# First convolution of each pass: one contiguous run over the padded rows instead of rows of 64 out of 66

## The chip, the cores and the metric

The kernel runs on one core of a Trainium2 chip. The metric is device time in microseconds (us), the median of several executions of the whole program. Engines are named as the profile names them: PE is TensorE's matmul, PEld its weight load, DVE is VectorE, ACT is ScalarE, POOL is GpSimd, SP is SyncE.

## The reference, cut to what matters

Three residual steps of two 3x3 convolutions with 64 channels on 16 images of 64 x 64, and behind them one attention block with matrix products of 64 channels. Only the two convolutions matter here:

```
for _ in range(3):
    t = relu(conv(x, w1) + b1)          # 3x3, SAME padding, 64 -> 64 channels
    x = x + 1/3 * (conv(t, w2) + b2)
return relu(x)
```

All is float32. The changed code computes `conv(x, w1)`, called conv0 below; `conv(t, w2)` is conv1.

## The kernel before, in words

**Layout.** An image has 32 groups of two rows each: the 64 channels of the even rows stand on partitions 0 to 63, those of the odd rows on partitions 64 to 127. A group has 64 columns. The tiles `x_hi` and `x_lo` hold an image in two parts (`x_hi` the value rounded to the fp32r type, `x_lo` what is left), with `PADDED` = 66 elements for each group: one zero, 64 pixels, one zero. So an image is 32 x 66 elements to a partition, with no hole between the groups.

**conv0** (`convolve_conv0`, on PE). The output `t` has 33 groups (`SKEWED`), shifted by one row against the groups of x. They are made in five parts of 7, 7, 7, 6 and 6 groups (`CONV0_SIZES`), each in one PSUM bank. A part sums over two stacks (the x group above and the one below) and over three columns xx = 0, 1, 2 of the filter. Each of these six takes three matmuls in the helper `three`: hi x hi, hi x lo and lo x hi (lines 889 to 891), so 18 matmuls a part. In the first part one stack has a group less (its x group lies outside the image), and so in the last part. A matmul before the change reads 64 of each 66 elements (7 rows of 64 with a pitch of 66, shifted by xx), and writes 7 x 64 = 448 contiguous elements of PSUM.

**What follows conv0.** ACT takes each part out of its bank through a ReLU into `t_eo` (`drain_conv0`, lines 488 to 493), even and odd columns apart. DVE turns `t_eo` into `v_all` in two sets (`transform_t`, lines 716 to 731): groups 0 to 20 after part 2, the rest after part 4. conv1 (line 930) multiplies `v_all` on PE, in fp32, in two halves: the first half needs only the first set. Its results go by ACT to `m`, by DVE to `dx`, by an accumulating DMA of POOL into `x_res`, and by ACT and DVE into `x_hi` and `x_lo` again.

**Order.** One round of the loop treats a pair of images, in six passes that alternate between the two images: conv0 in five parts, then conv1 in two halves (7 numbers a pass, `NC` = 42 in a round). There are 8 rounds, so 48 passes. Every engine runs its own instructions in program order and waits on semaphores. Between the convolutions of round i the attention of the pair before is put in by a table (`LATE`), by the number after which a piece comes. Its last pieces on ACT are the `FINISH` steps (line 561), which wait until a store from the same one of two output buffers is done (`stored`, line 387 issues the stores). The last of them stand at numbers 34 and 35, the end of the fifth pass and the first part of the sixth. The three banks for convolutions are used in turn, and PE waits with a part until ACT has emptied the bank three parts before (`bank_free`).

Of the kernel before, what the change touches and what calls it, by code (L numbers as in the profile page):

```python
# [35 lines left out]
IMAGES, CH, ROWS, COLS = 16, 64, 64, 64  # L36
# [8 lines left out]
PADDED = COLS + 2  # L45
# [31 lines left out]
def img_of(n):  # L77

    return PASS[n] % 2


def step_of(n):

    return PASS[n] // 2
# [17 lines left out]
def groups_of(n):  # L102

    if is_conv1(n):
        return half_of(n) * HALF_GROUPS, HALF_GROUPS
    return sum(CONV0_SIZES[:PART[n]]), CONV0_SIZES[PART[n]]


CONV_BANKS = 3
RING = 4  # L110
UNITS = [3 if is_conv1(n) else 1 for n in range(NC)]
UNIT = [sum(UNITS[:n]) for n in range(NC)]
# [67 lines left out]
def i_is(i, value):  # L180

    return isinstance(i, int) and i == value


def conv_attention_kernel(nc, x, w1, b1, w2, b2, qkv_w, o1_w, o2_w, kln_w, kln_b, vln_w, vln_b, out):
# [4 lines left out]
    with ctx:  # L190
# [6 lines left out]
        def pair_of(name, shape, dt=F32):  # L197
            return [sb(f"{name}{k}", shape, dt) for k in range(2)]
# [5 lines left out]
        x_hi = pair_of("x_hi", [P, GROUPS, PADDED], F32R)  # L204
        x_lo = pair_of("x_lo", [P, GROUPS, PADDED], F32R)
# [4 lines left out]
        m = pair_of("m", [P, 6 * PLANE])  # L210
# [49 lines left out]
        conv_ps = banks[0:CONV_BANKS]  # L260
# [177 lines left out]
        def _(act):  # L438
# [37 lines left out]
            def drain_conv0(i, n):  # L476
                g0, size = groups_of(n)
                act.wait_ge(conv_ready, i * NU + UNIT[n] + 1)
                if PART[n] == 0:
                    if i_is(i, 0) and n == 0:  # L480
                        act.wait_ge(consts_made, 3)
                    else:

                        act.wait_ge(v_made, i * NH + PASS[n] * HALVES)
                at = conv_ps[UNIT[n] % CONV_BANKS][:, 0:size * COLS].rearrange("p (j m s) -> p j s m", s=2, m=COLS // 2)
                to = t_eo[:, g0:g0 + size, :, 1:ROW - 1]
                if g0 == 0:
                    nc.scalar.activation(to[0:CH, 0:1], at[0:CH, 0:1], ACT.Relu, bias=b1_col[0:CH, :])
                    at, to = at[:, 1:size], to[:, 1:size]
                elif g0 + size == SKEWED:  # L490
                    nc.scalar.activation(to[CH:P, size - 1:size], at[CH:P, size - 1:size], ACT.Relu, bias=b1_col[CH:P, :])
                    at, to = at[:, 0:size - 1], to[:, 0:size - 1]
                nc.scalar.activation(to, at, ACT.Relu, bias=b1_col[:, :]).then_inc(drained, 1)  # L493
# [74 lines left out]
            def iteration(i, attends, splits, first=False):  # L568
                for n in range(NC):
                    if is_conv1(n):  # L570
                        drain_conv1(i, n)
                    else:
                        drain_conv0(i, n)
                    for number in REFRESH_AT[n]:
                        refresh_hi(i, number)
                    if not first:
                        for number in REFRESH_AT.get(NC + n, ()):
                            refresh_hi(i - 1, number)
                    if first:
                        set_up(n)  # L580
                    if attends:
                        attention(i - 1, LATE[n], RING_USES)
                    if not splits:
                        attention(i, EARLY_LAST.get(n, []), RING_LAST)
                    if splits and n in X_SPLIT[0]:
                        act.wait_ge(f_written, i * 2 * HALVES + HALVES)
                        copy_x(i + 1, 0, X_SPLIT[0][n])
                        split_x_hi(i + 1, 0, X_SPLIT[0][n])
                    if not first and n in X_SPLIT[1]:
                        act.wait_ge(f_written, i * 2 * HALVES)  # L590
                        copy_x(i, 1, X_SPLIT[1][n])
                        split_x_hi(i, 1, X_SPLIT[1][n])
# [266 lines left out]
        def _(pe):  # L859
# [27 lines left out]
            def three(ps, lhs, rhs, first, last):  # L887

                mm(ps, lhs[0], rhs[0], start=first, stop=False)  # L889
                mm(ps, lhs[0], rhs[1], start=False, stop=False)  # L890
                return mm(ps, lhs[1], rhs[0], start=False, stop=last)  # L891

            def convolve_conv0(i, n):
                img, step = img_of(n), step_of(n)
                g0, size = groups_of(n)
                if step == 0:

                    pe.wait_ge(x_split, i * 4 + 2 * img + 1 + (g0 + size >= HALF_GROUPS))
                else:

                    pe.wait_ge(x_ready, i * NR + (PASS[n] - 2) * HALVES + 1 + (g0 + size > HALF_GROUPS))
                bank_free(i, UNIT[n])
                hi, lo = x_hi[img], x_lo[img]
                top, bottom = g0 == 0, g0 + size == SKEWED
                for nth, stack in enumerate((1, 0) if top else (0, 1)):
                    skip_first, skip_last = int(top and stack == 0), int(bottom and stack == 1)
                    ps = conv_ps[UNIT[n] % CONV_BANKS][:, skip_first * COLS:(size - skip_last) * COLS]
                    groups = slice(g0 + stack - 1 + skip_first, g0 + stack - 1 + size - skip_last)
                    for xx in range(K):
                        at = stack * K + xx  # L910
                        cols = slice(xx, xx + COLS)
                        last = three(ps, (w_hi[:, at, :], w_lo[:, at, :]),
                                     (hi[:, groups, cols], lo[:, groups, cols]),
                                     nth == 0 and xx == 0, nth == 1 and xx == K - 1)
                last.then_inc(conv_ready, 1)

# [17 lines left out]
            def bank_free(i, unit):  # L934

                if not (i_is(i, 0) and unit < CONV_BANKS):
                    pe.wait_ge(drained, i * NU + unit - CONV_BANKS + 1)
# [102 lines left out]
            def iteration(i, attends, splits, first=False):  # L1040
                for n in range(NC):
                    if is_conv1(n):
                        convolve_conv1(i, n)
                    else:
                        convolve_conv0(i, n)
                    if first:
                        set_up(n)
                    if attends:
                        attention(i - 1, LATE[n], RING_USES)
                    if not splits:  # L1050
                        attention(i, EARLY_LAST.get(n, []), RING_LAST)
# [27 lines left out]
```

## Time and profile before

| | |
|---|---|
| median of 3 runs | 1622.37 us (1621.98 to 1623.78) |
| profiled execution, first to last instruction (its span) | 1619.8 us |
| PE busy | 1581.7 us, 98% of the span |
| PEld busy | 1372.0 us, 85% |
| DVE busy | 1090.7 us, 67% |
| ACT busy | 751.2 us, 46% |

The profile is of one execution. The page gives no other time for it than its span; the 2.6 us by which the median of the runs is longer lie before the first and behind the last instruction, and in the variation from run to run. Busy times of matmuls overlap, since one starts before the one ahead of it is through; what a stream of matmuls costs is read from the distance between starts.

### The profile page before, as it was taken

What the parts mean: (1) busy time and instruction counts of PE and PEld (TensorE: products, weight loads), DVE (VectorE), ACT (ScalarE), POOL (GpSimd) and SP (SyncE); (2) the same over time, 40 slices, a digit from 0 to 9 for tenths busy, and PEclk for the clock granted to TensorE, in tenths of its full rate; (3) what the DMA queues carried; (4) which work ended last, traced back from release to release, by engine and by line L of the source; (5) the groups of instructions that cost most, each with busy time, mean ns of one, the idle gap of its engine ahead of it and who ended that gap; (6) DMA issues with size and microseconds to landing.
All of it is one profiled execution on the core that took longest, in us unless ns stands there. A gap on an engine that the chain in (4) does not pass through costs nothing.

```text
span 1619.8 us, 25740 instructions
## 1 busy us (share of the span) xinstructions
PE 1581.7 (98%) x9339; PEld 1372.0 (85%) x9339; DVE 1090.7 (67%) x2060; ACT 751.2 (46%) x1322; POOL 85.9 (5%) x107
## 2 busy tenths in 40 slices
PE   7999999999999999999999999999999999999975
PEld 6999988888988889888898888988898879988862
DVE  5565687556875577765767667775587665876574
ACT  4333544436443464435643446433464334543454
POOL 0000000000000000000000000000000000000000
PEclk9999999999999999999999999999999999999997
DMA  6212332333322234122421235122531233112312
GB/s 114 53 26 53 53 53 40 62 57 53 66 40 53 53 55 77 27 52 53 80 52 27 52 66 92 27 39 49 90 60 27 40 59 59 27 27 53 69 37 52
DMA packets 149190, 85.98 MB, mean 53 GB/s; under 512 B 136652, under 2 KB 136652, under 8 KB 149068
## 3 DMA queue, kind: packets, MB, share of 16 engines
q0 software_dynamic: 13824, 50.34, 17.3%
q1 hardware_dynamic: 135164, 33.82, 11.3%
q8 instruction: 83, 1.36, 0.3%
q14 instruction: 39, 0.32, 0.1%
q10 hardware_dynamic: 80, 0.15, 0.0%
HBM read 17.17 MB, written 16.78 MB: 21 GB/s over the span
## 4 chain that ended last, share of the span: by engine, by line
PE 93%; DVE 3%; ACT 2%; issue 1%; DMA 1%; SPq 0%; ACTq 0%; DVEq 0%
PE bank L930 30%; PE bank L889 18%; PE bank L891 16%; PE bank L890 16%; PE bank L977 4%; PE bank L989 4%; PE bank L1023 2%; PE bank L1036 2%; DMA out<-y_out 0%; SPq L387 0%; PE bank L1007 0%; DVE rstd L791 0%; ACT g L541 0%; DVE x_lo L652 0%; ACT x_in L536 0%
## 5 line engine op out<-in xcount | busy, mean ns | idle before, releaser
L889 PE MATMUL bank<-x_hi,w_hi 128*128 128x448 f32 (+2 forms) x1440 | 526.3, 365 | 3.5 <-DVE x_lo L652 3.3
L930 PE MATMUL bank<-v_all,fw 128*128 128x256 f32 x2304 | 517.1, 382 | 1.0 <-DVE v_all L731 0.6
L891 PE MATMUL bank<-x_hi,w_lo 128*128 128x448 f32 (+2 forms) x1440 | 509.3, 354 | 0.0
L890 PE MATMUL bank<-x_lo,w_hi 128*128 128x448 f32 (+2 forms) x1440 | 508.6, 353 | 0.0
L930 PEld LDWEIGHTS bank<-v_all,fw 128*128 128x128 f32 x2304 | 431.7, 190 | 73.7 <-ACT m L506 9.7
L889 PEld LDWEIGHTS bank<-x_hi,w_hi 128*128 128x128 f32 x1440 | 272.0, 189 | 48.3 <-issue 22.8
L891 PEld LDWEIGHTS bank<-x_hi,w_lo 128*128 128x128 f32 x1440 | 271.5, 189 | 15.2
L890 PEld LDWEIGHTS bank<-x_lo,w_hi 128*128 128x128 f32 x1440 | 271.6, 189 | 13.6
L493 ACT ACTIVATE t_eo<-bank,b_col 128x384 f32<-128x384 f32 (+2 forms) x240 | 141.6, 590 | 301.5 <-PE bank L891 300.9
L716 DVE TENSOR_TENSOR steps_q<-t_eo 128x1344 f32<-128x1344 f32 x96 | 119.9, 1249 | 193.4 <-ACT t_eo L493 193.4
L506 ACT ACTIVATE m<-bank 128x512 f32<-128x512 f32 x192 | 114.2, 602 | 167.7 <-PE bank L930 167.6
L434 POOL DMA_DIRECT2D x_res<-dx x96 | 82.4, 859 | 1481.7 <-DVE dx L762 1481.7
L744 DVE TENSOR_TENSOR sums<-m 128x512 f32<-128x512 f32 x96 | 66.3, 691 | 129.7 <-ACT m L506 129.7
L773 DVE TENSOR_TENSOR x_lo<-x_res,x_hi 128x1024 fp32r<-128x1024 f32 x64 | 78.2, 1222 | 106.6 <-ACT x_hi L519 106.6
L784 DVE TENSOR_REDUCE rstd<-g 128x64 f32<-128x512 f32 x128 | 84.4, 680 | 33.9 <-ACT g L541 33.8
L536 ACT ACTIVATE kv<-bank 128x512 f32<-128x512 f32 x120 | 72.7, 606 | 19.7 <-PE bank L977 19.7
L509 ACT ACTIVATE m<-bank,b_third 128x256 f32<-128x256 f32 x96 | 46.1, 480 | 71.7 <-PE bank L930 71.6
L989 PEld LDWEIGHTS bank<-kv 128*65 128x65 f32 x960 | 68.3, 141 | 12.6 <-DVE kv L797 7.4
L541 ACT ACTIVATE g<-bank 128x512 f32<-128x512 f32 x128 | 78.5, 613 | 0.0
L797 DVE TENSOR_TENSOR kv<-kv,rstd 128x512 f32<-128x512 f32 x120 | 76.7, 677 | 0.0
L989 PE MATMUL bank<-kv 128*65 128x65 f32 x960 | 69.0, 225 | 7.0 <-DVE kv L797 7.0
L977 PE MATMUL bank<-kvw,f 64*128 64x128 f32 x1024 | 73.9, 288 | 0.6 <-ACT f L523 0.6
(104 smaller groups left out, 1358.8 us busy)
## 6 DMA issues: line engine op xcount, KB each, us to landing
x_res<-dx POOLq DMA_DIRECT2D x96, 512.0 KB, 4.6
x_in<-in_x SPq DMA_DIRECT2D x64, 256.0 KB, 7.3
out<-y_out SPq DMA_DIRECT2D x120, 128.0 KB, 2.7
out<-v_all SPq DMA_DIRECT2D x8, 128.0 KB, 2.7
x_res<-in_L_conv_w ACTq DMA_DIRECT2D x1, 144.0 KB, 2.8
x_res<-in_L_conv_w SPq DMA_DIRECT2D x1, 144.0 KB, 4.6
b_col<-in_L_conv_b SPq DMA_DIRECT2D x4, 0.2 KB, 2.8
g<-in_L_conv_o_w SPq DMA_DIRECT2D x3, 16.0 KB
```

Of the source, the lines that this page charges most:

```text
L434: nc.gpsimd.dma_start(x_res[img][:, HALF_PX * h:HALF_PX * (h + 1)], dx[h][:, :], accum_op=ALU.add).then_inc(x_added[h], 16)
L493: nc.scalar.activation(to, at, ACT.Relu, bias=b1_col[:, :]).then_inc(drained, 1)
L506: nc.scalar.activation(to[:, BANK * part:BANK * (part + 1)], bank[:, :], ACT.Copy, scale=H_STEP).then_inc(drained, 1)
L541: nc.scalar.activation(squares[k % 2][:, :], ps[:, :], ACT.Square).then_inc(proj_taken, 1)
L716: vec.tensor_tensor(q, later, earlier, ALU.subtract).then_inc(v_parts, 1)
L784: vec.tensor_reduce(rstd[img][:, k, :], squares[k % 2][:, :].rearrange("p (h d) -> p h d", d=HD), AX.X, ALU.add).then_inc(squares_summed, 1)
L889: mm(ps, lhs[0], rhs[0], start=first, stop=False)
L890: mm(ps, lhs[0], rhs[1], start=False, stop=False)
L891: return mm(ps, lhs[1], rhs[0], start=False, stop=last)
L930: last = mm(ps, fw[:, q, 1 - stack, :], v_all[:, KEPT.index(q), g0 + stack:g0 + stack + size, :], start=stack == 0, stop=stack == 1)
L977: last = mm(ps[:, KV * j:KV * (j + 1)], f[img][rows, at], kvw[rows, :], start=True, stop=True)
L989: last = mm(outer_ps, rows[:, at, :], rows[:, at + 1, :], start=(k == 0 and j == 0), stop=(k == PROJ - 1 and j == PX_BANK - 1))
```

## The change

conv0's matmuls read one run without holes and write one: for 7 groups 7 x 66 - 2 = 460 elements, for 6 groups 394, for 5 groups 328. The run starts at column xx of its first group. The results of the two elements between one group and the next are written to PSUM too, and nobody reads them. So a group now has a pitch of 66 in the bank (7 x 66 = 462 of its 512 elements), and ACT's instructions read 64 out of each 66. Number, order and waits of the instructions stay.

```diff
@@ drain_conv0 (ACT)
-                at = conv_ps[UNIT[n] % CONV_BANKS][:, 0:size * COLS].rearrange("p (j m s) -> p j s m", s=2, m=COLS // 2)
+                at = conv_ps[UNIT[n] % CONV_BANKS][:, 0:size * PADDED].rearrange(
+                    "p (j w) -> p j w", w=PADDED)[:, :, 0:COLS].rearrange("p j (m s) -> p j s m", s=2)
@@ convolve_conv0 (PE)
-                hi, lo = x_hi[img], x_lo[img]
+                hi, lo = (t[img].rearrange("p j w -> p (j w)") for t in (x_hi, x_lo))
                 top, bottom = g0 == 0, g0 + size == SKEWED
                 for nth, stack in enumerate((1, 0) if top else (0, 1)):
                     skip_first, skip_last = int(top and stack == 0), int(bottom and stack == 1)
-                    ps = conv_ps[UNIT[n] % CONV_BANKS][:, skip_first * COLS:(size - skip_last) * COLS]
-                    groups = slice(g0 + stack - 1 + skip_first, g0 + stack - 1 + size - skip_last)
+                    rows = size - skip_first - skip_last
+                    run = rows * PADDED - 2
+                    ps = conv_ps[UNIT[n] % CONV_BANKS][:, skip_first * PADDED:skip_first * PADDED + run]
+                    start = (g0 + stack - 1 + skip_first) * PADDED
                     for xx in range(K):
                         at = stack * K + xx
-                        cols = slice(xx, xx + COLS)
+                        run_at = slice(start + xx, start + xx + run)
                         last = three(ps, (w_hi[:, at, :], w_lo[:, at, :]),
-                                     (hi[:, groups, cols], lo[:, groups, cols]),
+                                     (hi[:, run_at], lo[:, run_at]),
                                      nth == 0 and xx == 0, nth == 1 and xx == K - 1)
```

The first place is on PE, in the first part of the first pass, where stack 1 (7 groups) goes over to stack 0 (6 groups). A row is line, operation, output and inputs, and partitions x elements of the moving operand. Before:

```order
L889 MATMUL bank<-x_hi,w_hi 128x448
L890 MATMUL bank<-x_lo,w_hi 128x448
L891 MATMUL bank<-x_hi,w_lo 128x448
L889 MATMUL bank<-x_hi,w_hi 128x384
L890 MATMUL bank<-x_lo,w_hi 128x384
L891 MATMUL bank<-x_hi,w_lo 128x384
```

After:

```order
L890 MATMUL bank<-x_hi,w_hi 128x460
L891 MATMUL bank<-x_lo,w_hi 128x460
L892 MATMUL bank<-x_hi,w_lo 128x460
L890 MATMUL bank<-x_hi,w_hi 128x394
L891 MATMUL bank<-x_lo,w_hi 128x394
L892 MATMUL bank<-x_hi,w_lo 128x394
```

Nothing moved; 448 became 460 and 384 became 394, and the lines are numbered one higher.

The second place is on PE too, at the end of the first pass: the last matmuls of conv0 (5 groups) and conv1 behind them. Before:

```order
L889 MATMUL bank<-x_hi,w_hi 128x320
L890 MATMUL bank<-x_lo,w_hi 128x320
L891 MATMUL bank<-x_hi,w_lo 128x320
L930 MATMUL bank<-v_all,fw 128x256 x24
L873 MATMUL bank<-ident,g 128x128
```

After:

```order
L890 MATMUL bank<-x_hi,w_hi 128x328
L891 MATMUL bank<-x_lo,w_hi 128x328
L892 MATMUL bank<-x_hi,w_lo 128x328
L933 MATMUL bank<-v_all,fw 128x256 x24
L874 MATMUL bank<-ident,g 128x128
```

320 became 328. conv1 stays as it was, 24 matmuls a pass in the program.

## Rows read from the trace of the kernel before

**Rows 1.** The page: busy time of each engine, share of the span, instructions.

```profile
PE 1581.7 (98%) x9339; PEld 1372.0 (85%) x9339; DVE 1090.7 (67%) x2060; ACT 751.2 (46%) x1322; POOL 85.9 (5%) x107
```

**Rows 2.** The page: chain that ended last, by engine and by line.

```profile
PE 93%; DVE 3%; ACT 2%; issue 1%; DMA 1%; SPq 0%; ACTq 0%; DVEq 0%
PE bank L930 30%; PE bank L889 18%; PE bank L891 16%; PE bank L890 16%; PE bank L977 4%; PE bank L989 4%; PE bank L1023 2%; PE bank L1036 2%; DMA out<-y_out 0%; SPq L387 0%; PE bank L1007 0%; DVE rstd L791 0%; ACT g L541 0%; DVE x_lo L652 0%; ACT x_in L536 0%
```

**Rows 3.** Waits of PE: line, what for, us in total, times, longest.

```profile
PE bank L989 <- DVE kv L797: 7.0, 2, 5.7
PE bank L930 <- DVE v_all L731: 0.6, 2, 0.4
```

**Rows 4.** Groups by line and shape: count, busy us, mean ns of one.

```profile
L930 PE MATMUL bank<-v_all,fw 128*128 128x256 f32 x2304 | 517.1, 382 | 1.0 <-DVE v_all L731 0.6
L889 PE MATMUL bank<-x_hi,w_hi 128*128 128x448 f32 x720 | 278.5, 387 | 3.5 <-DVE x_lo L652 3.3
L889 PE MATMUL bank<-x_hi,w_hi 128*128 128x384 f32 x576 | 202.8, 352 | 0.0
L889 PE MATMUL bank<-x_hi,w_hi 128*128 128x320 f32 x144 | 45.0, 313 | 0.0
L889 PEld LDWEIGHTS bank<-x_hi,w_hi 128*128 128x128 f32 x1440 | 272.0, 189 | 48.3 <-issue 22.8 <-ACT t_eo L493 4.9
```

**Rows 5.** Timeline of PE, first pass: start, us until its end, line, shape.

```profile
10.03 0.58 PE L890 MATMUL bank<-x_lo,w_hi 128*128 128x448 f32 x1
12.64 0.54 PE L891 MATMUL bank<-x_hi,w_lo 128*128 128x448 f32 x1
...
14.64 0.37 PE L889 MATMUL bank<-x_hi,w_hi 128*128 128x448 f32 x1
18.18 0.37 PE L891 MATMUL bank<-x_hi,w_lo 128*128 128x448 f32 x1
...
25.23 0.34 PE L889 MATMUL bank<-x_hi,w_hi 128*128 128x384 f32 x1
30.09 0.31 PE L889 MATMUL bank<-x_hi,w_hi 128*128 128x320 f32 x1
31.28 0.31 PE L891 MATMUL bank<-x_hi,w_lo 128*128 128x320 f32 x1
31.43 8.79 PE L930 MATMUL bank<-v_all,fw 128*128 128x256 f32 x40
```

**Rows 6.** Chain in order of time, first pass: start, us, line, count.

```profile
31.59 10.36 PE bank L930 x48
```

**Rows 7.** Windows in the first pass: busy us (count) by engine, then PEclk, DMA.

```profile
14.60:18.20 3.60, 3.60 (x20) 3.26 (x18) 1.46 (x2) 2.68 (x4) 0.00 (x0) 1.00 0.19 35
25.20:31.40 6.20, 6.20 (x37) 6.18 (x37) 5.67 (x11) 3.32 (x4) 0.00 (x0) 1.00 0.76 146
31.60:41.90 10.30, 10.30 (x48) 8.76 (x47) 7.27 (x22) 4.13 (x9) 0.40 (x1) 1.00 0.37 60
```

**Rows 8.** Timeline of DVE, first pass: transform of the first set, first and last.

```profile
26.17 1.55 DVE L716 TENSOR_TENSOR steps_q<-t_eo 128x1344 f32<-128x1344 f32 x1
...
30.08 0.85 DVE L731 SCALAR_TENSOR_TENSOR v_all<-steps_q 128x672 f32<-128x672 f32 x1
```

**Rows 9.** Timeline of a sixth pass (round 6 of 8), from its first matmul to conv1.

```profile
1134.40 0.48 PE L889 MATMUL bank<-x_hi,w_hi 128*128 128x448 f32 x1
1137.48 1.23 ACT L561 ACTIVATE y_out<-y 128x512 f32<-128x512 f32 x2 [1.76 <-DVE y L824]
1138.30 8.46 SPq L387 DMA_DIRECT2D out<-y_out  x6
1144.55 0.66 ACT L561 ACTIVATE y_out<-y 128x512 f32<-128x512 f32 x1 [5.19 <-DMA out<-y_out]
1145.37 0.66 ACT L561 ACTIVATE y_out<-y 128x512 f32<-128x512 f32 x1 [0.16 <-DMA out<-y_out]
1145.93 0.62 ACT L493 ACTIVATE t_eo<-bank,b_col 128x448 f32<-128x448 f32 x1
1146.44 1.05 ACT L523 ACTIVATE f<-x_res 128x1024 f32<-128x1024 f32 x1
1147.39 0.62 ACT L493 ACTIVATE t_eo<-bank,b_col 128x448 f32<-128x448 f32 x1
1148.05 1.56 DVE L716 TENSOR_TENSOR steps_q<-t_eo 128x1344 f32<-128x1344 f32 x1 [7.51 <-ACT t_eo L493]
1151.97 0.85 DVE L731 SCALAR_TENSOR_TENSOR v_all<-steps_q 128x672 f32<-128x672 f32 x1
1152.95 10.62 PE L930 MATMUL bank<-v_all,fw 128*128 128x256 f32 x48
```

**Rows 10.** Waits of ACT for stores: us in total, times, longest.

```profile
ACT y_out L561 <- DMA out<-y_out: 37.4, 11, 5.7
```

## The prediction

> **What bounds the kernel now.** I read the busy shares first, then the chain that ended last, then PE's waits, then the distance between the starts of matmuls. PE is busy for 98% of the span, DVE for 67%, ACT for 46% [rows 1]. The chain agrees: 93% of it is PE, and conv0's three lines hold 18 + 16 + 16 = 50% of it, some 810 us [rows 2]. PE waits for nearly nothing: its longest wait in total is 7.0 us, and for conv1's input it waits 0.6 us [rows 3]. So a nanosecond on a conv0 matmul counts 4320 times: each of the three lines has 720 matmuls of 448 elements, 576 of 384 and 144 of 320 [rows 4], which makes 2160, 1728 and 432.
>
> What one costs is the distance of starts [rows 5]:
> - 448 elements: from 14.64 to 18.18 are 17 steps, 208.2 ns each
> - 384: from 25.23 to 30.09 are 27 steps, 180.0 ns each
> - 320: from 30.09 to 31.28 are 8 steps, 148.8 ns each
> - conv1: 48 matmuls of 256 elements in 10.36 us, 215.8 ns each [rows 6]
>
> The granted clock is 1.00 in all these stretches [rows 7], the level of 2.4 GHz. The weight load does not set the distance: one takes 189 ns [rows 4], yet 320-element matmuls follow each other in 148.8. conv1 has 24 matmuls a pass in the program and 48 in the trace (2304 over 48 passes [rows 4]), so an fp32 matmul is run in two, and 256 elements in 215.8 ns are two array cycles an element (213.3 ns) and 2.5 ns over. This is a contiguous read, and it runs at the clock. conv0 does not: at one cycle an element, 448 elements would be 186.7 + 2.5 = 189.2 ns, and the row says 208.2. The excess is 19.0 ns for 7 rows, 17.5 for 6 (162.5 to 180.0), 13.0 for 5 (135.8 to 148.8): 2.6 to 2.9 ns a row.
>
> The Trainium skill's "TensorE: Matmul & The Clock Gate", section "Back-to-back issue gap", gives elements / 2.4 + 2.5 ns for one matmul at the full clock. By that rule the conv1 row agrees with two runs over its elements, and the conv0 row does not.
>
> **The open question.** All rows of conv0 have 64 elements, so the trace fits two readings equally well. In one, each of the 7 rows costs about 2.7 ns where the read jumps over the two pads. In the other, an fp32r element costs 0.46 ns instead of 0.417, in whatever pattern: (208.2 - 2.5) / 448 = 0.459, (180.0 - 2.5) / 384 = 0.462, (148.8 - 2.5) / 320 = 0.457. For the first speaks that the only contiguous stream, conv1, shows no excess; against it, that conv1 takes its elements at half the rate, so a limit of supply would not show there. In the first nine matmuls, from 10.03 to 12.64, 7 steps take 372.9 ns each [rows 5], just 448 elements at the lower level of 1.2 GHz with no excess (the level is read from the distance alone here). So the excess is no fixed number of array cycles; it lies in the supply, which both readings allow. I take the first, since a supply limited by its mere rate would be 0.459 / 0.417 = 1.10 times the array's cycle, a ratio for which I see no reason, where an interruption at each jump needs none.
>
> **The change part by part.**
> - *Elements added.* 12, 10 and 8 a matmul: 2160 x 12 + 1728 x 10 + 432 x 8 = 46,656. At 0.4167 ns, +19.4 us.
> - *Jumps removed.* In the first reading all excess goes: 2160 x 19.0 + 1728 x 17.5 + 432 x 13.0 ns = 41.0 + 30.2 + 5.6 = 76.8 us. Net -57.4 us, or 194.2 ns for 460, 166.7 for 394, 139.2 for 328. Bounds: nothing removed and the rate kept is 46,656 x 0.46 = +21.5 us; all removed is -57.4.
> - *ACT's read of the bank.* 64 out of each 66 instead of contiguous groups; it already steps by two elements, with as many instructions. I take zero. No row shows a pitch of 66 in PSUM. Were a 448-element read 0.1 us longer, a fifth of its 0.62 us [rows 9], ACT with 46% has room, except in the sixth passes (below), where two such reads and DVE's start behind them would cost some 0.2 us in each of six rounds, 1.2 us.
> - *What no longer hides.* DVE's transform of the first set runs under parts 3 and 4. In the first pass it ends at 30.08 + 0.85 = 30.93, and conv1 starts at 31.43 [rows 5, 8]: 0.50 us to spare. Parts 3 and 4 shrink by 27 x 13.3 + 9 x 9.6 ns = 0.45 us, so it is just hidden still; I charge nothing for the six passes of round 1. In the sixth pass of round 6 it is not hidden. ACT stands 5.19 us in a FINISH step until a store lands, drains part 1 at 1145.93 and part 2 only at 1147.39; DVE ends at 1152.82, and conv1 starts at 1152.95 [rows 9], 0.13 us later, about what a semaphore needs. This chain hangs on a DMA that was issued at 1138.30, near the start of the pass at 1134.40 [rows 9], and on work ahead of that start, not on PE's matmuls in between. What conv0 saves in this pass, 45 x 14.0 + 36 x 13.3 + 9 x 9.6 ns = 1.2 us, PE then waits at line 930. ACT waits for stores 37.4 us in all, 11 times [rows 10]: with 5.19 and 0.16 us in this pass, that is six passes of some 5.3 us and a remainder. They are those of rounds 2 to 7; in the first there is no attention beside the convolutions, and the eighth has another order. Loss 6 x 1.15 = 6.9 us. Lower bound of the loss: only what parts 3 and 4 save, 6 x 0.4 = 2.4 us.
>
> **Sum.** -57.4 + 6.9 = -50.5 us. The profiled execution's span is 1619.8 us, so its span should be 1569.3; the 2.6 us to the median of the runs stay, which gives 1572. Own range of this case: 1560 (the lower loss, 4.5 us less, and 1.7 ns a matmul more gained than the rounded starts show, 7.3 us) to 1585 (3 ns a matmul stay with the run, about the price of one jump, 4320 x 3 ns = 13 us).
>
> **Rivals.**
> 1. *The rate is the limit, not the jump (slower).* 46,656 elements more at 0.46 ns: +21.5 us, 1644. The point that decides is the distance of two 460-element starts: below 208.2 ns the change gains, and at this rate it is 460 x 0.459 + 2.5 = 213.6 ns. For it speaks the equal fit above, and that no contiguous fp32r read is in the trace; against it conv1's exact two cycles and the odd ratio. Chance 0.14.
> 2. *The jump costs only a part of the excess.* If half is rate and half jump, -76.8 / 2 + 19.4 = -19 us, with some 1 us lost at waits, 1604; this case reaches from 1585 to 1619. Chance 0.16.
> 3. *No net change.* The excess removed equals the elements added (a quarter of it removed): within 0.2%, which is 3.2 us and about what a measurement of this kernel can tell. Chance 0.03.
>
> 4. *The excess belongs to the matmul, not to its rows (slower).* Something at the change from one fp32r matmul to the next costs 13 to 19 ns, and stays; then only the added elements count, +19.4 us, 1642. Against it: the excess falls with the rows, 19.0, 17.5, 13.0, and is 0 in the first nine matmuls. Chance 0.04.
>
> The gap rule of "TensorE: Matmul & The Clock Gate" in the Trainium skill ("Back-to-back issue gap") goes with rival 4: it counts elements alone, whatever the pattern, so that 12 more can only cost 5 ns. The page "SBUF — State Buffer" in the Trainium skill, section "Specifications", says that each crossing to a new line of 16 bytes pays a penalty; a run of 460 crosses lines as the rows did, so by that rule too there is little to gain, as in rival 1. No row here tells crossings from jumps.
>
> **How the numbers follow.** The forecast case has 0.63, the partial one 0.16, no change 0.03, slower 0.14 + 0.04 = 0.18. The predicted time is that of the forecast case, 1572. The range takes in its own range and the partial case, 1560 to 1619, which holds 0.79. Faster by over 0.2% is 0.63 + 0.16 = 0.79, same 0.03, slower 0.18.
>
> **What the next profile would show.** Starts of 460-element matmuls 194 ns apart, of 394 167 and of 328 139: the first reading; 214, 184 and 153: the rate; 211, 182 and 152: rival 4. Waits of line 933 (conv1) for v_all of some 1.1 us in the sixth passes, near 7 us in all instead of 0.6. ACT's drains at 0.62 us as before. conv1 still at 215.8 ns. The prediction is wrong if a contiguous run keeps an excess that grows with its length, or if the shorter conv0 exposes DVE in more passes than the sixth.

## The result, and the profile after

The changed kernel takes 1625.15 us (median of 20 runs, 1623.38 to 1629.04) against 1622.38 us before (20 runs). The ratio is 1.0016, with a 95% interval of 1.001 to 1.0023: 2.6 us slower, and within the 0.2% that I called no change. I had forecast 1572 us, with a chance of 0.03 for this.

Ahead of everything else stands the distance of starts. Timeline of PE in the first pass of the changed kernel (start, us until its end, line, shape), the places of [rows 5]:

```profile
14.48 0.37 PE L890 MATMUL bank<-x_hi,w_hi 128*128 128x460 f32 x1
18.03 0.37 PE L892 MATMUL bank<-x_hi,w_lo 128*128 128x460 f32 x1
...
25.10 0.34 PE L890 MATMUL bank<-x_hi,w_hi 128*128 128x394 f32 x1
29.93 0.31 PE L890 MATMUL bank<-x_hi,w_hi 128*128 128x328 f32 x1
31.28 9.01 PE L933 MATMUL bank<-v_all,fw 128*128 128x256 f32 x41
```

From 14.48 to 18.03 are 17 steps, 208.8 ns each, where rows of 448 took 208.2. From 25.10 to 29.93 are 27 steps of 178.9 ns (180.0 before), and 9 steps of 150.0 ns to 31.28 (148.8 before). Forecast were 194.2, 166.7 and 139.2. The jumps are gone, and most of the excess is still there: 14.6, 12.2 and 10.8 ns above the forecast, of the 19.0, 17.5 and 13.0 that were to go. What a whole pass costs is read from the starts of conv1, in the chain that ended last, in order of time (start, us, line, count). Before, and behind it the changed kernel, three passes between the two lines of each:

```profile
87.45 10.36 PE bank L930 x48
170.13 10.36 PE bank L930 x48
```

```profile
87.39 10.36 PE bank L933 x48
170.21 10.36 PE bank L933 x48
```

conv1 takes 10.36 us in both, as in [rows 6]. A pass takes 27.56 us before and 27.61 after, so the 90 matmuls of conv0 in it cost 0.05 us more (0.14 over the three passes). Over 48 passes that would be 2.2 us, an estimate from these three, and nearly the whole of the 2.6 us.

The page of the changed kernel, busy time of each engine:

```profile
PE 1585.9 (98%) x9339; PEld 1374.2 (85%) x9339; DVE 1090.1 (67%) x2060; ACT 750.9 (46%) x1322; POOL 85.9 (5%) x107
```

Against [rows 1] PE is busy 4.2 us longer, DVE and ACT as long to 0.6 us. The span is 1622.7 us, 2.9 more than before. PE's waits for conv1's input, among the waits of PE (us in total, times, longest), and ACT's drain of 448 elements, among the groups by line and shape:

```profile
PE bank L933 <- DVE v_all L732: 0.2, 1, 0.2
```

```profile
L494 ACT ACTIVATE t_eo<-bank,b_col 128x448 f32<-128x448 f32 x96 | 61.0, 636 | 178.4 <-PE bank L892 178.4
```

The waits that I expected behind a shorter conv0 are not there, since conv0 is not shorter (0.2 us, 0.6 in [rows 3]). The drain with a pitch of 66 takes 636 ns, the same group before 635.

### The profile page after: what moved, and what is told of

Same layout as the page of the kernel before. It is cut to its first block, busy times and chain, and to the rows that moved or that the text cites. A ratio compares the mean times of both kernels' runs of the same rounds, so it can differ in the third digit from the quotient of the medians.

```text
span 1622.7 us, 25740 instructions
## 1 busy us (share of the span) xinstructions
PE 1585.9 (98%) x9339; PEld 1374.2 (85%) x9339; DVE 1090.1 (67%) x2060; ACT 750.9 (46%) x1322; POOL 85.9 (5%) x107
## 4 chain that ended last, share of the span: by engine, by line
PE 93%; ACT 3%; DVE 2%; issue 1%; DMA 0%; SPq 0%; ACTq 0%; DVEq 0%
PE bank L933 30%; PE bank L890 18%; PE bank L891 16%; PE bank L892 16%; PE bank L992 4%; PE bank L980 4%; PE bank L1026 2%; PE bank L1039 2%; ACT g L542 1%; PE bank L1010 0%; DVE rstd L792 0%; DVE x_lo L653 0%; ACT kv L537 0%; ACT x_in L537 0%; ACT f L524 0%
## 5 line engine op out<-in xcount | busy, mean ns | idle before, releaser
L890 PE MATMUL bank<-x_hi,w_hi 128*128 128x460 f32 (+2 forms) x1440 | 527.2, 366 | 3.4 <-DVE x_lo L653 3.3
L891 PE MATMUL bank<-x_lo,w_hi 128*128 128x460 f32 (+2 forms) x1440 | 510.6, 355 | 0.0
L892 PE MATMUL bank<-x_hi,w_lo 128*128 128x460 f32 (+2 forms) x1440 | 510.4, 354 | 0.0
L892 PEld LDWEIGHTS bank<-x_hi,w_lo 128*128 128x128 f32 x1440 | 272.0, 189 | 15.1
```

## The experiments

Whole kernels are compared with the kernel before. A difference in us is the ratio times the time before; the difference of the two medians is up to 1.6 us off it (in e3), within the interval. In three programs (e1, e4, e11) PE runs stretches of 36 matmuls and no other engine computes. A first stretch, whose first nine matmuls stand some 373 ns apart, goes ahead and is not counted; behind it the granted clock is 1.00. These programs leave out the whole computation and store a copy of x, and those stores run beside the stretches until about 110 us.

My theory after the result (R): an fp32r element has a price of supply above one array cycle, whatever the pattern, and a row end costs a little more; the 12 elements added then cost what the 6 jumps had cost. Against it stand W (the write into PSUM), P (power of the data), D (other engines' traffic) and my reading on record (the jump).

### e1: forms of read by themselves

The loop in outline; the program writes each stretch out:

```diff
+# one stretch; a and b give the moving operand (rows, or a run), at element 66 * (k // 18) + k // 3 % 3
+for k in range(36):
+    mm(banks[k // 18 % 3][:, 0:n], w[:, 128 * (k % 6):128 * (k % 6) + 128],
+       (b if k % 3 == 1 else a)(66 * (k // 18) + k // 3 % 3), start=k % 18 == 0, stop=k % 18 == 17)
```

> No convolution kernel: PE alone issues 34 stretches of 36 matmuls, each stretch one form of read, with nothing running beside it. Read is the mean distance of starts. Theory R (an fp32r element costs about 0.453 ns to supply, in whatever pattern, and a row end a little more): runs of 256, 320, 384, 448, 512 at 118, 147, 176, 205, 234 ns, the same with zeros as data and with 64 columns of weights; bf16 at 189 ns for 448, zero excess. Theory W (the write of one fp32 result a cycle into PSUM is the limit): bf16 448 also at 205 to 208. Theory P (the array's clock gives way under the power of fp32r data): zeros at 189, random data at 208, bf16 between. Theory D (other engines' traffic, or what surrounds the matmuls in the whole kernel): all forms at elements / 2.4 + 2.5 ns here, 189 for 448 both in rows and as a run. My own reading on record (a jump costs 2.7 ns): a run of 448 at 189 and rows of 64 at 208, rows of 8 in 10 far above.

The chain that ended last, in order of time. Lines 91 (rows of 64 in 66), 95 (run of 460), 99 (448), 103 (512), 107 (384), 111 (256), 119 (320), 131 (394):

```profile
25.85 7.53 PE bank L91 x36
33.38 7.49 PE bank L95 x36
40.87 7.35 PE bank L99 x36
48.22 8.35 PE bank L103 x36
56.57 6.26 PE bank L107 x36
62.83 4.31 PE bank L111 x36
...
71.94 5.30 PE bank L119 x36
...
88.50 6.46 PE bank L131 x36
```

Divided by 36: rows of 64 in 66 209.2 ns, runs of 460, 448, 512 208.1, 204.2, 231.9, and of 384, 256, 320, 394 173.9, 119.7, 147.2, 179.4. Between 256 and 512 that is (231.9 - 119.7) / 256 = 0.438 ns an element and 7.6 ns besides. So a contiguous fp32r run has an excess of its own: 204.2 for 448, where 448 / 2.4 + 2.5 is 189.2. Of these 15.0 ns some 9.5 grow with the elements (448 x 0.021) and some 5 do not (7.6 against 2.5). Rows cost 5.0 ns more than the run of as many elements, for 6 jumps 0.83 ns each. The stores run beside all of these; four stretches without them follow. Lines 155 (run of 448, each matmul a sum of its own), 159 (rows of 64 in 72), 163 (64 in 128), 219 (64 in 66 again):

```profile
128.53 7.31 PE bank L155 x36
135.84 7.68 PE bank L159 x36
143.52 7.63 PE bank L163 x36
...
288.34 7.50 PE bank L219 x36
```

Windows of the same trace, over lines 95 and 155: busy us (count) by engine, then PEclk, DMA share, GB/s:

```profile
33.40:40.80 7.40, 7.40 (x37) 6.67 (x37) 0.00 (x0) 0.00 (x0) 0.00 (x0) 1.00 0.89 194
128.60:135.80 7.20, 7.20 (x37) 6.67 (x36) 0.00 (x0) 0.00 (x0) 0.00 (x0) 1.00 0.00 0
```

With the DMA engines idle a run of 448 takes 203.1 ns and rows of 64 in 66 take 208.3, against 204.2 and 209.2 with 194 GB/s of stores. So the excess is there without other traffic (D falls), and the same form repeats to about 1 ns, which leaves the jump at 0.8 ns give or take 0.2. Rows further apart cost more: 213.3 ns in 72 and 211.9 in 128, some 1.5 and 1.3 ns a jump over 204.2. The 0.8 ns is the price of skipping two elements.

The chain in order of time again, lines 167 (rows of 32 in 34), 171 (16 in 18), 175 (8 in 10), 179 and 183 (zeros as data: rows of 64, run of 448), 187 (bf16, run of 448), 191 (bf16, rows of 64 in 66), 199 and 203 (fp32, run of 448 and rows), 211 (fp32r, 32 columns of weights):

```profile
151.15 7.71 PE bank L167 x36
158.86 8.11 PE bank L171 x36
166.97 8.97 PE bank L175 x36
175.95 7.51 PE bank L179 x36
183.45 7.35 PE bank L183 x36
190.80 6.84 PE bank L187 x36
197.64 6.88 PE bank L191 x36
...
212.30 27.06 PE bank L199 x72
239.36 27.06 PE bank L203 x72
...
273.76 7.28 PE bank L211 x36
```

With 13, 27 and 55 jumps in 448 elements a matmul takes 214.2, 225.3 and 249.2 ns, again 0.8 ns a jump over 204.2, each over two elements. bf16 takes 190.0 as a run and 191.1 in rows, about the array's 189.2; so neither the array nor the write of one result a cycle is the limit (theory W falls). Zeros take 208.6 and 204.2 like other data (P falls). 32 columns of weights take 202.2, though their load lasts 108 ns instead of 188 (98 in bf16), so the weight load explains 2 ns at most. fp32 takes 375.8 ns for two cycles an element, with jumps or without. Theory R stands, with a rate of 0.438 instead of 0.453.

### e2: the pitch of 66 in PSUM alone

```diff
-ps = conv_ps[...][:, skip_first * COLS:(size - skip_last) * COLS]
+ps = conv_ps[...][:, skip_first * PADDED:(size - skip_last) * PADDED].rearrange("p (j w) -> p j w", w=PADDED)[:, :, 0:COLS]
 # ACT's read as in the change; the matmuls still read rows of 64 out of 66
```

> One part of the change alone: results are written with a pitch of 66 in PSUM and read so by ACT, but the matmuls still read rows of 64 out of 66, so 448 elements each. Theory R, supply at the read side: as before, within 0.1%. If the pitch in PSUM costs anything in the write or in ACT's read: up to 0.3% slower, the whole of what the change lost.

Ratio 0.9996, interval 0.9987 to 1.0006: the write with a pitch and ACT's read of it cost nothing that shows. What the change lost is on the read side of PE.

### e3: runs without the added elements

```diff
-(hi[:, groups, cols], lo[:, groups, cols])
+(hi[:, start:start + 64 * rows], lo[:, start:start + 64 * rows])    # flat; start = 66 * first group + xx
```

> The other part alone, and without the added elements: a matmul reads one run of 64 elements for each row (448, 384, 320), without jumps, so what it multiplies is not the convolution's pixels from the second row on. Theory R: 205.5 ns for 448 instead of 208.2, 3 ns x 4320, so 10 to 13 us faster than before, 0.7%. My own reading on record (a jump costs 2.7 ns): 70 us faster. If the distance does not depend on jumps or on a few elements: no change.

Ratio 0.9912, interval 0.9898 to 0.9926: 14.3 us faster (12.0 to 16.6). From the second row on it reads other elements than the convolution needs. 23,328 jumps are gone (2160 x 6 + 1728 x 5 + 432 x 4), which at 0.83 ns makes 19.4 us. Part of it came back as waits, the first of the kind that the prediction spoke of. Waits of PE:

```profile
PE bank L932 <- DVE v_all L731: 3.3, 6, 0.7
```

3.3 us in 6 times, where [rows 3] had 0.6 us in 2. With these 2.7 us the gain at the matmuls is 17.0 us, 0.73 ns a jump. The passes say nearly the same: three take from 88.86 to 170.52, 27.22 us each against 27.56 before, which over 48 is 16.3 us or 0.70 ns a jump. Both are near e1's 0.8 and far from my 2.6 to 2.9.

### e4: type, bytes spanned, first element

As e1, with other stretches:

```diff
+b_hi[:, s:s + 896].rearrange("p (j w) -> p j w", w=2)[:, :, 0:1]      # bf16, every second element: 4 bytes apart
+b_hi[:, s:s + 1792].rearrange("p (j w) -> p j w", w=4)[:, :, 0:1]     # bf16, every fourth: 8 bytes apart
+x_hi[:, s:s + 896].rearrange("p (j w) -> p j w", w=2)[:, :, 0:1]      # fp32r, every second: 8 bytes apart
```

> PE alone again, 22 stretches of 36 matmuls. Asked: what the excess of fp32r hangs on. Theory R (supply by the element: 8.4 ns + 0.436 ns an element, fitted to the ten runs of the stretches before): 454 elements at 206.5, 472 at 214.3, 192 at 92, rows of 64 in 65 as rows of 64 in 66 (some 208). If the place of the first element counts (lines of some size), the stretches that begin always at element 0, 4, 8, 16 stand below those from 1, 2, 3. If bytes spanned are the limit, and not the type: bf16 that takes every second element (4 bytes apart) stands at the 204 ns of an fp32r run, and every fourth at twice that or so; if the type is the limit: both stay at 189. With 64 partitions as with 128: 204.

The chain in order of time. Lines 127 (run of 454), 139 (472), 143 (192), 151 and 155 (bf16, every second, every fourth), 159 (bf16, run of 448), 163 (fp32r, every second):

```profile
91.91 7.54 PE bank L127 x36
...
114.22 7.72 PE bank L139 x36
121.94 4.00 PE bank L143 x36
...
129.93 7.17 PE bank L151 x36
137.09 14.25 PE bank L155 x36
151.34 6.82 PE bank L159 x36
158.16 14.26 PE bank L163 x36
```

Lengths: 472 took 214.4 ns, as expected (214.3), and 454 took 209.4, where 206.5 was expected. bf16 with its elements 4 bytes apart takes 199.2 ns, ten of the 15 ns by which fp32r's run stands above bf16's 189.4. With 8 bytes between elements bf16 takes 395.8 and fp32r 396.1, 0.88 ns an element, twice the 0.438. So the limit follows the bytes spanned, at about 0.88 ns for 8 bytes, and mostly not the type. Two fp32r elements are 8 bytes, and at the 0.417 ns of bf16's run they would take 0.833 ns; the shortfall is some 10 of the 15 ns at 448 elements. The Trainium skill's "SBUF — State Buffer", section "Door 1: The DMA port swizzle", in its note on cachelines, says that one may stride for free as long as two accesses fall in a line of 16 bytes, up to 4 fp32 or 8 bf16 elements; elements 8 bytes apart have two in such a line and cost double here. On PE's read the measurement decides against it. 192 elements, expected at 92 ns, took 111.1, and 128 took 110.8 (line 147): there something else is the floor, and what it is was not separated (the weight load, which lasts 192 ns there and overlaps the next, is a candidate). Two more forms: rows of 64 in 65 took 207.2 ns, as expected, and a run of 448 on 64 partitions took 211.9 (line 123), where 204 was expected; why it is longer than on 128 partitions was not followed up.

### e5: one zero between groups

```diff
-PADDED = COLS + 2
+PADDED = COLS + 1
+LEAD = 2                                       # elements ahead of the first group
 ...                                            # tiles, zeros and starts moved to fit
-run = rows * PADDED - 2
+run = rows * PADDED - 1 + (rows * PADDED - 1) % 2
```

> The change with fewer elements added: one zero between two groups instead of two, so runs of 454, 390 and 324 instead of 460, 394 and 328. Theory R: 206.5, 178.6 and 149.8 ns, against 208.5, 179.9 and 149.7 before: 2160 x 2.0 + 1728 x 1.3 = 6.6 us faster than before (0.4%), 9 faster than the change. If instead only the count of matmuls or something else at their borders sets the distance: as before.

Ratio 0.9955, interval 0.9942 to 0.9969: 7.3 us faster than before, 9.9 faster than the change, which has 21,600 elements more (0.46 ns each). conv1 waits 1.4 us for `v_all`, in 4 times. The odd run of 389 is made 390.

### e6: bf16 instead of fp32r

```diff
-F32R = mybir.dt.float32r
+F32R = mybir.dt.bfloat16
 ...                                            # four casts of these tiles to fp32 dropped
```

> The kernel before with bf16 in place of fp32r for both parts of x and of the first filter, still three products and rows of 64 in 66; the sum is a little less exact. Theory R (supply of 4-byte elements is the limit): 191, 164 and 138 ns a matmul, which takes 69.7 us from PE; of that the sixth passes of rounds 2 to 7 give 6 x 1.4 = 8.5 us back in waits for v_all, as the prediction says of its own gain. So -61 us, 3.8% faster, and some 8 us of waits of line 930. If the waits hide nothing: -70. If the array or PSUM is the limit: no change.

Ratio 0.9638, interval 0.9624 to 0.9653: 58.7 us faster, 61 expected. The output is of this split of x and w1 into two bf16 parts, less exact than fp32r's. Groups of PE by line and shape, and its wait for conv1's input:

```profile
L930 PE MATMUL bank<-v_all,fw 128*128 128x256 f32 x2304 | 519.5, 383 | 13.8 <-DVE v_all L731 10.1 <-ACT m L511 3.3 <-issue 0.4
```

```profile
PE bank L930 <- DVE v_all L731: 10.1, 6, 1.9
```

conv1 now waits 10.1 us in six times for `v_all`, as the prediction had it for a conv0 that is really shorter (6.9 us for its own gain, 8.5 for this one). Some smaller waits of the attention's chain grow too (line 1004 for `kv_head`, 5.4 us instead of 1.6).

### e7: four zeros between groups

```diff
-PADDED = COLS + 2
+PADDED = COLS + 4
-run = rows * PADDED - 2
+run = rows * PADDED - 4
 ...                                            # all four zeros are written
```

> The change with more elements added: four zeros between groups, so runs of 472, 404 and 336. Theory R: 214.3, 184.7 and 155.0 ns, 23 us slower than before (1.4%), 20 slower than the change. If added elements were free up to a point, as the result of the change would also allow: as before.

Ratio 1.0141, interval 1.0126 to 1.0157: 22.9 us slower than before, 20.3 slower than the change. That is another 46,656 elements, 0.435 ns each.

### e8 and e9: who makes conv1 of the sixth pass wait

```diff
 for _k, _gap in enumerate(_gaps):
-    LATE[_gap] += steps(_kind, _img, _k) + (steps(FINISH, _img, _k) if _kind == DOWN else [])
+    LATE[_gap] += steps(_kind, _img, _k)
+    if _kind == DOWN:
+        LATE[38 if _gap == 35 else _gap] += steps(FINISH, _img, _k)
```

> The bf16 kernel (1565.09 us), with the FINISH steps of number 35 moved to number 38 on ACT, so that ACT no longer stands before a store's landing while parts 1 and 2 of the sixth pass wait to be drained. If that wait is what conv1 of the sixth pass pays (10.1 us of waits for v_all in 6 passes, the prediction's mechanism): those waits nearly go, 8 to 10 us faster than the bf16 kernel, 1556, ratio to before 0.958. If the late transform has another cause: 1565, with the 10.1 us still there.

> The kernel before with the same move of the FINISH steps alone. Its conv1 waits 0.6 us for v_all in all, so there is nothing to give back: within 0.1% of before. If ACT's wait costs PE in another way already (banks not drained in time): up to 5 us faster.

On bf16 (e8): ratio 0.9574, interval 0.9561 to 0.9587, 69.1 us faster than before and 10.4 more than e6. conv1's waits in e8, groups of PE by line and shape:

```profile
L932 PE MATMUL bank<-v_all,fw 128*128 128x256 f32 x2304 | 517.8, 382 | 3.4 <-ACT m L513 3.3
```

The 10.1 us for `v_all` are gone, and so are ACT's waits for stores, which in e6 stood as

```profile
ACT y_out L561 <- DMA out<-y_out: 37.9, 14, 5.6
```

On the kernel before (e9): ratio 1.0004, interval 0.9995 to 1.0013, no change, as expected. ACT's waits for stores are gone here too (37.4 us in [rows 10]). So they cost nothing while conv0 is slow, and some 10 us once it is fast.

### e10: the change on bf16

The change and e6's edit together.

> The change itself (runs of 460, 394, 328) on bf16. If in bf16 an element costs 0.417 ns and a jump nearly nothing, as the stretches showed (run of 448 189.5, rows of 64 in 66 191.3): 194, 167 and 139 ns against 192, 165 and 137.5 of the bf16 rows, so 9 to 10 us of PE more, 8 to 9 us slower than the bf16 kernel with rows: 1573 to 1574, ratio to before 0.969. If the excess of fp32r were in the jumps after all: no slower than the bf16 rows.

Ratio 0.9685, interval 0.967 to 0.9699: 51.1 us faster than before, but 7.6 slower than rows on bf16 (e6). Where elements come at the array's rate and a jump costs next to nothing, added elements are a plain loss: 46,656 x 0.417 = 19.4 us at most, less what rows cost in bf16 and what the waits give back (v_all 8.6 us instead of 10.1). Three passes take from 88.28 to 167.57 here and from 83.87 to 162.64 in e6, 26.43 and 26.26 us each: 0.17 us more, 8.3 us over 48 passes, close to the 7.6 measured. Groups of PE by line and shape:

```profile
L933 PE MATMUL bank<-v_all,fw 128*128 128x256 f32 x2304 | 517.5, 382 | 11.3 <-DVE v_all L732 8.6 <-ACT m L512 2.7
```

### e11: the first element

```diff
+x_hi[:, o:o + 448]        # fp32r, one tile, o = 0 to 15, one stretch each; then other forms
```

> PE alone, fp32r, one tile: a run of 448 that begins at each of the elements 0 to 15, then with one weight tile for all, then runs of 512. Asked: whether the 10 ns between starts of the stretches before (200 to 210) follow the place of the first element. If lines of 16 bytes count: a period of 4, with 0, 4, 8, 12 lowest. If lines of 32 or 64 bytes: a period of 8 or 16. If it hangs on the distance between moving data and weights: other values with one weight tile. If none of them: no period, and the mean over all stays at 204, so that the excess over 189 is not a matter of the first element.

The chain in order of time; lines 91, 95, 99, 103, 107 begin at elements 0, 1, 2, 3, 4, lines 119, 135 and 151 at 7, 11 and 15, lines 155 and 159 at 0 and 1 with one weight tile:

```profile
25.86 7.29 PE bank L91 x36
33.16 7.54 PE bank L95 x36
40.70 7.43 PE bank L99 x36
48.13 7.20 PE bank L103 x36
55.34 7.21 PE bank L107 x36
...
77.40 7.20 PE bank L119 x36
...
106.86 7.26 PE bank L135 x36
...
136.24 7.20 PE bank L151 x36
143.44 7.43 PE bank L155 x36
150.87 7.44 PE bank L159 x36
```

Starts at 3, 4, 7 and 15 take 200.0 to 200.3 ns, 0 takes 202.5, 1 takes 209.4; the mean of all sixteen is 204.1. The low points do not lie at the multiples of 4, 8 or 16, but a period of 4 elements, 16 bytes, does show: starts 3, 7, 11 and 15 take 200.0 to 201.7, and those that leave 1 or 2 when divided by 4 take 204.4 to 209.4 (the multiples of 4 lie between, 200.3 to 206.7). e4, with two tiles, has 200.0 at start 3 and 209.4 and 206.4 at 1 and 2. With one weight tile start 0 takes 206.4 and start 1 206.7, and starts 3 and 4 take 200.0 and 200.3 (lines 163 and 167). So the start moves the distance by up to 5 ns either way, and never down to 189. At its best, 200.0, little is left beside the rate (448 x 0.438 + 2.5 = 198.7); the 5 ns that e1 found besides the rate may be this effect, which is not shown.

## Why the prediction was wrong

**What bounds the kernel** was right: conv0's matmuls are on the path. e7 and e5 move the time by 20.3 and -9.9 us against the change, with the elements alone.

**The step that failed** is "The open question", and with it the term "Jumps removed". I had two readings that fitted equally, and took the jumps, because a rate of 1.10 cycles an element seemed to have no reason. Of the 19.0 ns of excess at 448 elements, e1 puts some 15 on the run itself (9.5 on the rate at which fp32r elements come, 5 that do not grow with them) and 4 to 5 on the 6 jumps. Only the jumps went, and a matmul takes 208.8 ns instead of 208.2, since 12 added elements cost what the jumps had cost. So the term of -76.8 us should have been 23,328 jumps at 0.8 ns, about -19 us (-16 by e3's passes), a quarter of it. The chance of 0.03 stood at just that quarter (rival 3). That the sum comes out near zero is an accident of two pads to a row: with one or four it does not (e5, e7). My row for the first reading, conv1 at exactly two cycles, could not decide, as the prediction itself had allowed: e1's fp32 stretches show that at half the rate neither jumps nor the element's size are felt (375.8 ns in both forms). The first nine matmuls, 372.9 ns apart, hid the excess in the same way; their level of 1.2 GHz is read from that distance, for the profile's granted clock reads 1.00 over them too.

The sum, redone with e1's prices (0.438 ns an element, 0.83 a jump; 0.417 in bf16), against what was measured:

| kernel | elements added | worked out, us | measured, us |
|---|---|---|---|
| the change | 46,656 | +20.4 - 19.4 = +1.0 | +2.6 |
| e3, run of 448 | 0 | -19.4 | -14.3, with 2.7 of waits in it |
| e5, pitch 65 | 25,056 | +11.0 - 19.4 = -8.4 | -7.3, with 0.8 of waits in it |
| e7, pitch 68 | 93,312 | +40.9 - 19.4 = +21.5 | +22.9 |
| e10 against e6 | 46,656 | +19.4 - 4.3 = +15.1 | +7.6, with 1.5 less of waits in it |

The 4.3 us are 23,328 jumps at bf16's 0.18 ns. With e3's 0.70 ns a jump the change comes to +4.1, so the two prices enclose the measured +2.6 (1.6 to 3.7) and neither gives it alone. The 5 ns that do not grow with the elements are in no row of the table, since the number of matmuls is the same. e10 comes out at half of what is worked out, and why is not shown; part of it is that a stretch of conv1 takes 10.40 us in e10 and 10.49 in e6.

**Elements added** was right in kind (+19.4 us forecast at the array's rate; 20.4 at the measured one). It was paid in full, while what it was to buy was mostly not there to be bought.

**ACT's read of the bank** at nothing was right: e2 shows none, and the drain takes 636 ns after against 635 before.

**What no longer hides** was right as a mechanism, and did not come into play, since the conv0 of the change is no shorter. e3, e6 and e10 show it in 6 passes each, the sixth ones of rounds 2 to 7 as forecast (3.3, 10.1 and 8.6 us), with 8.5 expected for e6. e8 and e9 show its cause, ACT in front of a store.

**Rivals.** Rival 1 (the rate is the limit) was right in its cause, and wrong in its price, because it left the jumps at nothing: the rows that fitted 0.46 were 0.438, the jumps and some 5 ns a matmul together. Rival 4 falls in the main: most of the excess grows within the run, by the element, and bf16 has none; some 5 ns do belong to the matmul. The starts that I gave for rival 4 (211, 182) do not follow from its own excess, which gives 213, 184 and 152, too near rival 1's 214, 184 and 153 to tell the two apart. The rule that I weighed, "TensorE: Matmul & The Clock Gate" of the Trainium skill ("Back-to-back issue gap"), given there for a matmul by itself, holds here in streams of bf16 (189.4 for 448) and for fp32's two cycles an element (375.8 against 373.3 + 2.5), and not for fp32r.

**Open.** Why 8 bytes take 0.88 ns instead of 0.83, why the start of a run moves this by up to 5 ns either way, with a period of 4 elements, and why a jump over 8 or 64 elements costs more than one over two, is not settled.

## What to carry to other kernels

Where two readings of a row fit equally, an argument from tidiness decides nothing: a stretch of a few matmuls of each form would have answered before the forecast, and the range should have held both. An access pattern with holes costs by the hole and a run by what it reads on top: at 0.8 ns a jump and 0.44 ns an element, filling a hole of two elements breaks even. Against rows with holes of two, runs with one pad gain and runs with four lose (e5, e7). Against rows with a hole of one, a run was not seen to gain: in e4 rows of 64 in 65 take 207.2 ns and the run of 454 takes 209.4. A fast stream takes its price from the bytes that it spans: two bf16 parts instead of two fp32r parts took 3.6% off this kernel, where they are exact enough, and moving one ACT step out of the way of the drains gave another 0.6%, though the same step cost nothing before.

## What the runs showed of the hardware

- fp32r does not stream at the array's rate at 2.4 GHz: 7.6 ns and 0.438 ns an element for runs of 256 to 512 (204.2 ns for 448). bf16 takes 0.417 an element and 2.5: 189.4 ns for 448.
- The limit is in bytes spanned: 4 bytes apart bf16 takes 199.2 ns for 448, 8 bytes apart 395.8, and fp32r 8 bytes apart 396.1.
- It is not power (zeros 204.2), not the weight load (32 columns, loaded in 108 ns: 202.2), and not other traffic (203.1 with the DMA engines idle, 204.2 with 194 GB/s of stores).
- A jump over two elements in the read of an fp32r operand costs 0.8 ns whether the rows have 64, 32, 16 or 8 elements, and over 8 or 64 elements 1.5 and 1.3; in fp32 (over two) it costs nothing, in bf16 about 0.2 ns.
- The first element of an fp32r run of 448 counts with a period of 4: starts 3, 7, 11 and 15 take 200.0 to 201.7 ns, starts 1, 5, 9 and 13 take 205.3 to 209.4.
- 128 and 192 fp32r elements both take 111 ns.
